# A decoder layer on one Trainium2 core: the stacked operands of each attention head by way of device memory

## What is computed

```python
q = x @ Wq; k = x @ Wk; v = x @ Wv
latent = (k + v) @ W_down_kv
qh, kh, vh = heads(q), heads(latent @ W_up_k), heads(latent @ W_up_v)   # (B, 16, S, 16)
scores = einsum('bhqd,bhkd->bhqk', qh, kh) * scale
decay = exp(-0.01 * 0.01 * abs(i - j))
out = einsum('bhqk,bhkd->bhqd', softmax(scores * decay), vh)
x = x + out.transpose(0, 2, 1, 3).reshape(B, S, D) @ Wo
```

## Time and profile before

| | |
|---|---|
| median of 3 runs | 841.52 us (841.37 to 843.31) |
| the profiled execution | 846.5 us |
| its span in the profile | 844.7 us |
| busy: PE, ACT, DVE, POOL | 659.7, 401.3, 352.8, 226.8 us |
| DMA packets | 66.50 MB, mean 79 GB/s |
| stage of the heads | 124.7 to about 399 us |

### The profile page before, as it was taken

One profiled execution on the slowest core, in us unless ns is written; L12 is line 12 of the kernel. 1 busy time (PEld: TensorE's weight loads), 2 busy tenths in 40 slices (PEclk: granted clock), 3 DMA queues, 4 the chain that ended last, 5 costly groups with the idle time before them and its releaser, 6 DMA issues.

```text
span 844.7 us, 14905 instructions
## 1 busy us (share of the span) xinstructions
PE 659.7 (78%) x4414; PEld 370.4 (44%) x4415; DVE 352.8 (42%) x1005; ACT 401.3 (48%) x503; POOL 226.8 (27%) x245
## 2 busy tenths in 40 slices
PE   0899519999999999998687899996646288888950
PEld 0444203444444444443554566665623155555530
DVE  2329953434434433333242555552451133333353
ACT  2144228999999999999122333331500022222100
POOL 2034608919708900000100000000037400000365
PEclk9999858999999999999698999995659599999975
DMA  9600035555555555553640000000002223333335
GB/s 291 220 0 0 1 52 84 91 93 95 90 95 92 95 93 96 90 96 76 183 117 0 1 0 1 0 0 0 1 31 104 89 81 112 106 111 106 93 106 157
DMA packets 55379, 66.50 MB, mean 79 GB/s; under 512 B 10994, under 2 KB 46964, under 8 KB 55348
## 3 DMA queue, kind: packets, MB, share of 16 engines
q1 hardware_dynamic: 52276, 57.73, 30.7%
q0 software_dynamic: 3072, 8.39, 3.2%
HBM read 22.04 MB, written 18.87 MB: 48 GB/s over the span
## 4 chain that ended last, share of the span: by engine, by line
PE 49%; SPq 14%; DVE 12%; issue 11%; DMA 7%; another core or an unknown queue 2%; ACT 2%; DVEq 1%; POOL 1%; POOLq 0%; ACTq 0%
SPq L347 12%; PE ps L639 8%; PE ps L912 6%; PE ps L651 6%; DMA kstack<-parts 5%; PE ps L786 4%; PE ps L766 3%; PE ps L927 3%; PE ps L538 3%; PE ps L736 2%; PE ps L800 2%; PE ps L531 2%; PE ps L904 1%; PE ps L801 1%
## 5 line engine op out<-in xcount | busy, mean ns | idle before, releaser
L639 PE MATMUL ps<-qstack,kstack 96*128 96x512 bf16 (+3 forms) x704 | 135.7, 327 | 17.1 <-DMA kstack<-parts 16.2
L1357 DVE TENSOR_TENSOR ps<-ps,within 128x128 f32<-128x128 f32 x256 | 75.7, 296 | 165.0 <-PE ps L639 160.5
L1059 ACT ACTIVATE pT<-ps,shift 128x1024 f32<-128x1024 f32 x128 | 136.9, 1124 | 16.0 <-PE ps L639 13.7
L639 PEld LDWEIGHTS ps<-qstack,kstack 96*128 96x128 bf16 x704 | 58.4, 98 | 89.4 <-ACT xn L1059 22.0
L651 PE MATMUL ps<-pT,vcur 128*32 128x256 f32 x1024 | 80.9, 389 | 0.0
L1059 ACT ACTIVATE xnT<-ps,shift 128x1024 f32<-128x1024 f32 x64 | 71.7, 1120 | 0.0
L1059 ACT ACTIVATE xn<-ps,shift 128x1024 f32<-128x1024 f32 x64 | 71.5, 1118 | 0.0
L514 POOL DMA_INDIRECT val<-y_slots,place_i x32 | 31.3, 977 | 141.2 <-DMA y_slots<-ftmp 127.6
L912 PE MATMUL ps<-parts,oT 128*128 x192 | 55.3, 413 | 17.2 <-ACT oT L1175 12.3
L506 POOL DMA_INDIRECT x_slots<-val,place_i x32 | 31.5, 984 | 87.0 <-DVE place_i L1577 77.5
L1180 ACT ACTIVATE xnT<-ps 128x128 f32<-128x128 f32 x48 | 13.3, 277 | 78.9 <-PE ps L912 78.9
(11 more groups left out here) (237 smaller groups left out, 1131.4 us busy)
## 6 DMA issues: line engine op xcount, KB each, us to landing
qstack<-parts SPq DMA_DIRECT2D x192, 64.0 KB, 2.3
kstack<-parts SPq DMA_DIRECT2D x192, 64.0 KB, 2.4
x_slots<-wcur SPq DMA_DIRECT2D x1, 6144.0 KB, 20.6
kT<-x_slots SPq DMA_DIRECT2D x48, 128.0 KB, 2.0
y_slots<-ftmp SPq DMA_DIRECT2D x48, 128.0 KB, 1.7
resid<-in_x_dram SPq DMA_DIRECT2D x4, 512.0 KB, 5.3
parts<-in_L_ffn_Wg_dram SPq DMA_DIRECT2D x16, 128.0 KB, 2.3
parts<-in_L_ffn_Wu_dram SPq DMA_DIRECT2D x16, 128.0 KB, 2.2
```

What stands on the lines that cost most here:

```text
L639: mm = nc.tensor.matmul(ps[:, score_bank(g3, kt) + g, a - lo:z - lo], kstack[:, r, 1 - sign, kt * P:(kt + 1) * P], qstack[:, r, sign, a:z] ...
L1059: nc.scalar.activation(pT_ring[kt % 4], two_banks(score_bank(g3, kt)).rearrange("p a n -> p (a n)"), ACT.Exp, bias=shift[:]).then_inc(s_ex ...
L1357: nc.vector.tensor_tensor(blk, blk, within[:], ALU.mult).then_inc(s_diag, 1)
```

## The change

`parts` no longer goes straight to the stacks. There is a new tensor in device memory, `stacks_d`, of [4 units, q or k, 768 rows, 2048] bf16, in the order in which the stacks want their rows: row 6p + i is row i of the six of partition p. `store_parts(u, lo, hi, stored)` writes partitions lo to hi of a unit into it with six DMAs: for q three, which write part 0 three times, part 1 twice and part 2 once (`Q_ROWS`, read with a repeat), for k three, which write parts 0 to 2, 0 to 1 and 0 (`K_ROWS`). `load_head` then fills each stack with one DMA of 96 partitions of 4 KB, so two for a head (`NB = 2`). The rows of a head stand in another order than before, the same in both stacks.

Unit 0 is stored in two pieces, partitions 0 to 31 before head 0's load and 32 to 127 behind head 1's. Units 1 to 3 are stored in two halves of 64 partitions, in the SP program at head 6 of unit 0 and at head 4 of units 1 and 2, behind that head's load; SP waits there for `s_parts`. Loads wait for `s_store_lo` or `s_store_hi` where a new piece begins.

```diff
-PRODUCTS = ((0, 0, 0, 1, 1, 2), (0, 1, 2, 0, 1, 0))
-NB = 2 * (SROWS // HD)
+Q_ROWS = ((0, 3, 0), (3, 2, 1), (5, 1, 2))
+K_ROWS = ((0, 3), (3, 2), (5, 1))
+NB = 2
+NS = len(Q_ROWS) + len(K_ROWS)
...
+            def store_parts(u, lo, hi, stored):
+
+                rows = stacks_d[u].rearrange("t (p r) n -> t p r n", r=NPROD)
+                part = parts[lo:hi, u % 2, :, :, :, :].rearrange("p t c v s -> p t c (v s)")
+                for r, n, c in Q_ROWS:
+                    sp.dma_start(rows[0, lo:hi, r:r + n, :], part[:, 0, c:c + 1, :].to_broadcast([hi - lo, n, 2 * S]))\
+                        .then_inc(stored, 16)
+                for r, n in K_ROWS:
+                    sp.dma_start(rows[1, lo:hi, r:r + n, :], part[:, 1, 0:n, :]).then_inc(stored, 16)
...
                 after(sp, s_fs, 2 * ST * (u * HH + j - 1))
-                head = parts[j * HD:(j + 1) * HD, u % 2, :, :, :, :]
                 for t, stk in ((0, qstack), (1, kstack)):
-                    for row in range(NPROD):
-                        sp.dma_start(stk[row * HD:(row + 1) * HD, r, :, :], head[:, t, PRODUCTS[t][row], :, :])\
-                            .then_inc(s_stack[r], 16)
+                    sp.dma_start(stk[:, r, :, :].rearrange("p v s -> p (v s)"),
+                                 stacks_d[u, t, j * SROWS:(j + 1) * SROWS, :]).then_inc(s_stack[r], 16)

             sp.wait_ge(s_parts0, 1)
+            store_parts(0, 0, 2 * HD, s_store_lo)
             sp.wait_ge(s_sums, 2)
+            sp.wait_ge(s_store_lo, 16 * NS)
             load_head(0, 0)
             load_head(0, 1)
+            store_parts(0, 2 * HD, P, s_store_hi)
...
                 for u in range(UNITS):
-                    sp.wait_ge(s_parts, u + 1)
                     for j in range(HH):
                         if u * HH + j >= 2:
+                            if j == 0:
+                                sp.wait_ge(s_store_lo, 16 * NS * (u + 1))
+                            if j == (2 if u == 0 else HH // 2):
+                                sp.wait_ge(s_store_hi, 16 * NS * (u + 1))
                             load_head(u, j)
+                        if j == (HH - 2 if u == 0 else HH // 2) and u + 1 < UNITS:
+                            sp.wait_ge(s_parts, u + 2)
+                            store_parts(u + 1, 0, P // 2, s_store_lo)
+                            store_parts(u + 1, P // 2, P, s_store_hi)
...
                 for u in range(1, UNITS):
-                    for r in range(2):
-                        after(pool, s_stack[r], 16 * NB * (HH // 2) * (u - 1))
+                    after(pool, s_store_lo, 16 * NS * (u - 1))
+                    after(pool, s_store_hi, 16 * NS * (u - 1))
```

More of the change, by code:

```diff
@@ L227, in decoder_layer @@
         wtop = sb("wtop", [P, TILES, TOPK])
+        stacks_d = nc.dram_tensor("stacks_d", [UNITS, 2, P * NPROD, 2 * S], BF16, kind="Internal").ap()
         x_slots = nc.dram_tensor("x_slots", [SLOT_TILES * P, D], F32, kind="Internal").ap()
@@ L254, in decoder_layer @@
         s_grow = sem("s_grow"); s_split = sem("s_split"); s_split0 = sem("s_split0"); s_parts = sem("s_parts")
-        s_parts0 = sem("s_parts0")
+        s_parts0 = sem("s_parts0"); s_store_lo = sem("s_store_lo"); s_store_hi = sem("s_store_hi")
         s_stack = [sem("s_stack0"), sem("s_stack1")]
@@ L484, in _ @@
                 pool.wait_ge(s_parts0, 1)
-                for r in range(2):
-                    pool.wait_ge(s_stack[r], 16 * NB)
+                pool.wait_ge(s_store_lo, 16 * NS)
+                pool.wait_ge(s_store_hi, 16 * NS)
                 nc.gpsimd.iota(diff_i, pattern=[[-1, 1920]], base=S - P, channel_multiplier=1).then_inc(s_decay, 1)
```

## The result

The change made the kernel slower: 904.22 us median of 4 runs (900.26 to 906.45) against 842.41 us before, a ratio of 1.073 (95% interval 1.068 to 1.078). The profiled execution took 902.18 us with a span of 900.4 us, 55.7 us above that of before.

The account below looks back on a forecast made before the run. SP's issuing of loads was taken as the limit of every second head in the heads' stage. 0.7 + 17.7 + 2 x 17.8 + 4.8 - 8.7 = +50.1 us on 841.5 gives 892 us; own range 878 to 906, 8-in-10 range 847 to 908.

Parts of the forecast that it names:

- start of head 2: Start of the stage: head 2 starts at 144.6 instead of 143.92 us, behind unit 0's store of 96 partitions; +0.7 us.
- wait at head 7: Unit 1's store, placed at head 6: head 7's load lands at 203.1, wanted at 185.4; PE waits 17.7 us.
- waits at heads 13 and 21: Stores of units 2 and 3: PE stands 17.8 us each, the next head's load landing behind the stores.
- slow clock behind these three: Heads behind the three long stalls run at the lower clock: 3 x 1.6 = +4.8 us, nothing if the clock holds.
- steady waits gone: Heads 2 to 31: with shorter loads on an empty queue, steady waits vanish, (8.46 - 8.16) x 29 = -8.7 us.
- I take 213: Rate in GB/s assumed for 64-partition stores, from a row with 64 partitions as the other end; 29.5 us a unit.
- The rival of full width: Stores run at 370 GB/s, 17 us a unit, with shorter stalls: 850 us; chance 18 in 100.
- a load issued behind 29.5 us of stores lands behind them: On SP's queue the next head's load does not get past a unit's stores; it lands 2.8 us after their data.
- Issuing them takes 12 x 0.6 = 7.5 us of SP: SP's time to issue a unit's twelve stores, 7.5 us, which alone would be hidden.
- landings of 25 us behind the stores: Sign of a right forecast: loads behind the stores land at 25 us, elsewhere at 3 to 4.
- landings under 8 us: Sign of a wrong forecast: loads behind the stores land in under 8 us.
- The faster rival: A head's load gets past the stores, so PE never stands: 828 to 834 us, 830 us; chance 11 in 100.

Follow-up runs that it names:

- Experiment 2: Changed kernel with units 1 to 3 stored by six DMAs of 128 partitions instead of twelve of 64; 1.025 of the kernel before, some 863 us.
- experiment 7: Against experiment 5: unit 0's q part stored by 128 partitions as soon as DVE has made it; 826.29 us, 0.986 of the kernel before.
- experiment 5: Changed kernel with each later unit's stores in four bursts of 1.57 MB, 128 partitions wide, behind four heads' loads; 0.9955 of the kernel before, some 839 us.
- experiments 2 to 4: Changed kernel with, in turn: stores 128 partitions wide (1.025); second six stores two heads later (1.022); stores from POOL's queue (1.030 of the kernel before).

## Why the prediction was right

It forecast 892 us, slower, by the mechanism that the runs bear out. Point by point, with the terms of its sum beside the profile (us):

| term | forecast | measured |
|---|---|---|
| start of head 2 | +0.7 | +3.1 (146.98 - 143.92) |
| slow clock behind that wait | not forecast | +2.8 (head 2 lasts 10.99, a free head 8.16) |
| wait at head 7 | +17.7 | +20.4 (28.53 - 8.16) |
| waits at heads 13 and 21 | +35.6 | +39.2 (19.6 each) |
| slow clock behind these three | +4.8 | +6.8 (1.6, 2.3 and 3.0) |
| steady waits gone | -8.7 | -8.4 (what is left to 63.9) |
| stage of the heads | +50.1 | +63.9 |

**The rate.** "I take 213": the stores ran at 220 GB/s alone. The choice by the one row with 64 partitions at one end was right, although it was a load and not a store. By the Trainium skill (SBUF — State Buffer, Door 1) partitions 0 to 63, or 64 to 127, reach half the ports. The rates agree with it for these stores, 220 against 422 GB/s; the ports themselves stand in no trace. The rival of full width at 850 us, the first in the list, fell with it. Experiment 2, which is that rival made real, came out at about 863, 13 us above its price, mostly because it leaves the start as it is (head 2 at 148.1 us; the rival, with full width there too, had forecast 139.0); its waits in the loop were 19.7 us in all where the rival had 20.8, with three slow heads behind them and not one.

**The order.** "a load issued behind 29.5 us of stores lands behind them": shown by the landing of 15.1 us in experiment 2. In the changed kernel itself a second thing did the same work, which I had not seen: "Issuing them takes 12 x 0.6 = 7.5 us of SP" was wrong (the product is 7.2), it took 26.3, and head 7's load was not even issued before 200.83. So a sign that I had named for the right mechanism, landings of 25 us behind the stores, did not come, and one that I had named for a wrong one, landings under 8 us, did: the loads of kstack at heads 7, 13 and 21 landed 7.1 to 7.7 us after so late an issue. The longest landing of all is one at the start:

```profile
DMA to landing us min/median/max: 4.0/4.5/8.4
```

It seems to have made no large difference to the end: the DMA engines were 97% busy through the wait at head 7, so the bytes took that time in any case. No run frees SP and keeps the stores of 64 partitions in one burst on its queue, so the two are not separated there.

**What was mis-sized.** Three small steps carry the 14 us between 50.1 and 63.9. A burst with its load was 36.7 us from the first store's issue to the landing of kstack (174.46 to 211.11) where 1.4 + 29.5 + 2.8 made 33.7: 2 to 3 us, three times. The start: head 0 came at 123.7, the store of 96 partitions landed at 141.8 instead of 140.0, and the load behind it took 5.0 us to the landing and not 4.4. And the clock: I had it fall behind the three long waits alone; it also fell around the 6 us at head 2. That wait was another of my signs of a wrong forecast, and the forecast itself held the half of it: its starts of heads 1 and 2, 132.9 and 144.6, are 3.5 us further apart than a free head. The mechanism was right, and each term came out on the slower side: 904 lies inside the 878 to 906 of the forecast's own range by only 2 us.

**The gain.** Heads 8.16 us apart, as forecast, nearly wherever the queue is empty. The faster rival named the right place: what it said overtaking would give (828 to 834 us), experiment 7 gets without overtaking, 0.986 of 842.41 being 830. The short bursts alone give 839 (experiment 5); the rest comes from the earlier store of unit 0's q part.

On the scale of the whole kernel the profiled execution was 55.7 us longer and not 63.9, because the stretch behind the heads was 8.2 us shorter in it; the medians differ by 61.8.

## What to carry to other kernels

A prefetch that must land within one step stands behind everything that was issued before it on its queue, so price a bulk store by the bytes it puts ahead of the next prefetch, at the rate of its own shape, and not by its issues or its mean share of the engines. Stored in four pieces, each short enough for the load behind it to land in time, 6.29 MB a unit made no later head wait here (one wait of 0.57 us at half width), where one burst cost PE 20 us at half width and 6 to 7 at full. Look also at when the first of the data exists: storing unit 0's q part 21 us earlier brought the last head forward by another 10.9 us (387.66 to 376.79).

## What the runs showed that I had not expected

In the changed kernel SP's issue of a DMA took 0.3 to 0.6 us on an empty queue, and 2.0 to 2.6 us from the third store of 64 partitions of a burst on, the load behind the burst included; with stores of 128 partitions it was 1.8 us at most. It does not go by the size of the DMA: stores of 0.26, 0.52 and 0.79 MB took about the same. On the mean a store is 0.52 MB, which at 220 GB/s is 2.4 us (an estimate), so a burst was issued about as fast as the engines worked it off. Nor does the number under way decide alone, for at the start six stores of 96 partitions went out in 0.4 to 0.8 us each, behind the loads of heads 0 and 1, of which the last landed only at 128.5:

```profile
L348 SPq DMA_DIRECT2D stacks_d<-parts x3: 428/464/505, 120.6 to 121.5; - x3
L351 SPq DMA_DIRECT2D stacks_d<-parts x3: 502/732/771, 122.1 to 123.4; - x3
```

What does decide stays open.

Short waits of PE are followed by a slow head too. Behind the 6.1 us at head 2 the granted clock was 0.71 on the mean of the window, and in experiments 2 to 4 each head behind a wait of 4 to 7 us lasted 9.7 to 11.0 us instead of 8.16.

The load of kstack for head 7, on SP's queue with the stores on POOL's, landed in 12.3 us: between the 3.9 to 5.1 us that it takes alone and the 15.1 us behind full-width stores on the same queue.
